# First experts of a two-layer block on one core: the up product with its operands exchanged, weights copied by VectorE, rows loaded four tiles ahead

## The reference, cut to what matters

```python
def _L0_ffn_ref(x, W1, b1, W2, b2, Wr, br):      # D, F, E = 256, 512, 8; x has 16 * 112 rows
    router_logits = jnp.einsum('bsd,de->bse', x, Wr) + br
    expert_idx = jnp.argmax(router_logits, axis=-1)
    h = jax.nn.relu(jnp.einsum('bsd,edf->ebsf', x, W1) + b1[:, None, None, :])
    y = jnp.einsum('ebsf,efd->ebsd', h, W2) + b2[:, None, None, :]
    onehot = jax.nn.one_hot(expert_idx, E, dtype=x.dtype)
    return jnp.einsum('ebsd,bse->bsd', y, onehot)
```

## Time and profile before

| | us |
|---|---|
| median of 3 runs (lowest, highest) | 850.89 (850.41, 851.85) |
| the profiled execution, its own time | 858.4 |
| span of its trace, first to last instruction | 856.7 |
| busy in the span: PE, PEld, DVE, ACT, POOL | 736.0, 543.2, 426.1, 325.7, 215.4 |
| mean granted TensorE clock, as a share of 2.4 GHz | 0.920 |

### The profile page before, as it was taken

The page is one execution under the profiler, slowest core; times in us unless marked ns, Lnnn a source line. Parts: engine busy times, 40 slices in busy tenths (PEclk is TensorE's granted clock), DMA queues, the critical chain, the costliest instruction groups (busy, mean ns, idle before and its releaser), DMA issues. The chain is left out here.

```text
span 856.7 us, 19046 instructions
## 1 busy us (share of the span) xinstructions
PE 736.0 (86%) x6340; PEld 543.2 (63%) x6341; DVE 426.1 (50%) x1316; ACT 325.7 (38%) x883; POOL 215.4 (25%) x362
## 2 busy tenths in 40 slices
PE   4589999999999999988865998873988983999996
PEld 3345667677776766665544565552766762899995
DVE  2455777777777777756621222222566764011111
ACT  2224665556555665544431322231444441111110
POOL 2301233322233233311100122222344432011111
PEclk9877999999999999999876899995999995899999
DMA  4999877788999888859332466703555531599960
GB/s 142 141 129 148 111 119 113 114 144 143 142 155 153 101 145 144 136 84 191 106 111 74 146 196 190 215 17 98 159 157 162 174 116 55 171 334 330 340 213 14
DMA packets 98086, 127.09 MB, mean 148 GB/s; under 512 B 23370, under 2 KB 82995, under 8 KB 97880
## 3 DMA queue, kind: packets, MB, share of 16 engines
q1 hardware_dynamic: 89926, 114.53, 62.4%
q0 software_dynamic: 3824, 8.46, 3.8%
q10 hardware_dynamic: 4258, 3.09, 1.5%
HBM read 74.68 MB, written 22.96 MB: 114 GB/s over the span
## 5 line engine op out<-in xcount | busy, mean ns | idle before, releaser
L491 ACT ACTIVATE probs<-psum 128x448 f32<-128x448 f32 (+2 forms) x256 | 125.4, 541 | 71.7 <-PE psum L772 70.7
L650 DVE TENSOR_REDUCE neg_max<-psum 112x2 f32<-112x750 f32 x128 | 119.0, 929 | 17.3 <-PE psum L755 15.3
L755 PE MATMUL psum<-stacks 96*128 96x487 bf16 (+1 forms) x256 | 79.7, 395 | 8.8 <-DMA stacks<-q_parts 7.5
L772 PE MATMUL psum<-stacks 102*128 102x112 bf16 (+1 forms) x1024 | 80.2, 219 | 8.0 <-DMA stacks<-mt 6.6
L772 PEld LDWEIGHTS psum<-stacks 102*128 102x128 bf16 (+1 forms) x1024 | 56.2, 101 | 40.0 <-ACT probs L491 21.3
L787 PE MATMUL psum<-probs,rings 128*32 128x112 f32 (+2 forms) x2048 | 79.5, 273 | 0.7 <-issue 0.7
L787 PEld LDWEIGHTS psum<-probs,rings 128*32 128x32 f32 (+2 forms) x2048 | 46.9, 112 | 48.7 <-issue 34.6
L1901 PEld LDWEIGHTS psum<-e_xt,rings 128*128 128x128 f32 x512 | 62.5, 200 | 2.3 <-ACT e_xt L1848 1.4
L1901 PE MATMUL psum<-e_xt,rings 128*128 128x112 f32 x512 | 62.7, 283 | 0.9 <-ACT e_xt L1848 0.9
L1915 PE MATMUL psum<-rings,e_hid 128*112 128x256 f32 x256 | 57.9, 379 | 1.3 <-DVE e_hid L1875 1.3
L1868 DVE SCALAR_TENSOR_TENSOR e_y<-psum,e_x_in 112x256 f32<-112x256 f32 x16 | 7.7, 484 | 97.9 <-PE psum L1915 97.9
(11 more groups left out here) (225 smaller groups left out, 1366.4 us busy)
## 6 DMA issues: line engine op xcount, KB each, us to landing
rings<-in_L_ffn_w SPq DMA_DIRECT2D x32, 1024.0 KB, 7.4
stacks<-rings SPq DMA_DIRECT2D x96, 243.5 KB
ct_dram<-rings SPq DMA_DIRECT2D x16, 375.0 KB, 11.0
a_ct<-ct_dram SPq DMA_DIRECT2D x16, 375.0 KB
a_ctx<-in_ctx SPq DMA_DIRECT2D x16, 375.0 KB
stacks<-q_parts SPq DMA_DIRECT2D x96, 56.0 KB
rings<-in_ctx SPq DMA_DIRECT2D x16, 256.0 KB
w<-in_L_ffn_W SPq DMA_DIRECT2D x8, 512.0 KB, 11.5
```

The costliest lines, as they stand in the source:

```text
L491: nc.scalar.activation(probs[k % 4][0:keys, :, :], src, ACT.Exp, scale=DH ** -0.5).then_inc(s["exp_done"], 1)
L650: nc.vector.tensor_reduce(neg_max[:, 0, h:h + 2], psum[0:T, pair:pair + 2, 0:S], AX, ALU.max, negate=True)
L755: last = nc.tensor.matmul(bank[2 - 2 * (k % 2) + j][0:rows, 0:KV], q_flat[n.third][0:QK, h * T:h * T + rows], k_stack[n.third][0:QK, h, :] ...
L772: last = nc.tensor.matmul(bank[4 + k % 2][0:wide, j * T:(j + 1) * T], k_flat[n.third][:, first:first + wide], q_stack[n.third][:, h, :], s ...
```

## The change

The up product exchanges its operands: the weights are stationary, the tokens move. The result then has the hidden axis on partitions and the turning back, its copy and a stage of the pipeline are gone. The stationary blocks are read from a copy `w1_now` that VectorE makes for each tile from the expert's weights (128 partitions, 1024 values), one tile ahead. The up result takes two banks of PSUM for each parity, `up` counts twice for each tile, and ScalarE makes the first half of `t_hid` after the first count. ScalarE now makes `t_hid` of tile j ahead of the copy of tile j+1. The down product, its bias and the scatter follow one step behind, not two, and there is one step less. Rows are loaded four tiles ahead into four buffers.

```diff
-        s_in = [g.sem(f"f0_tile_loaded{p}") for p in range(2)]
+        s_in = [g.sem(f"f0_tile_loaded{k}") for k in range(4)]
...
-            x_in = [tb(f"t0_in{p}", [P, ROW0]) for p in range(2)]
+            x_in = [tb(f"t0_in{k}", [P, ROW0]) for k in range(4)]
-            up = [tb(f"t0_up{p}", [P, F0]) for p in range(2)]
+            w1_now = [tb(f"t0_w1_{p}", [P, 2, F0]) for p in range(2)]
-            end = TILES + 2
+            end = TILES + 1
+            def up_bank(j, f):
+                return bank[4 * j.parity + f // 2]
...  SP
-                        if (j - 2).real():
-                            sp.wait_ge(s["x_mm"], (j - 2).count(1, 1))
+                        if (j - 4).real():
+                            sp.wait_ge(s["x_mm"], (j - 4).count(1, 1))
+                            sp.wait_ge(s["index_ready"], (j - 4).count(1, 1))
...
-                        if (j + 2).real():
-                            load(j + 2)
+                        if (j + 4).real():
+                            load(j + 4)
...  POOL
-                        if (j - 2).real():
-                            n = j - 2
+                        if (j - 1).real():
+                            n = j - 1
...  ACT
                     def step(j):
+                        if j.real():
+                            e = act.value_load(owner_i[0:1, j.at()], min_val=0, max_val=E0 - 1)
+                            if (j - 2).real():
+                                act.wait_ge(s["down"], (j - 2).count(1, 1))
+                            for f in range(K2):
+                                if f % 2 == 0:
+                                    act.wait_ge(s["up"], j.count(2, 1 + f // 2))
+                                bias = b1[:, bass.ds(e, 1), f:f + 1].rearrange("p o f -> p (o f)")
+                                nc.scalar.activation(hid[j.parity][:, f, :], up_bank(j, f)[:, f % 2 * P:(f % 2 + 1) * P], ACT.Relu,
+                                                     bias=bias).then_inc(s["hid"], 1)
                         if (j + 1).real():
                             copy_in(j + 1)
...  DVE
+                    def take_weights(j):
+                        e = dve.value_load(owner_i[0:1, j.at()], min_val=0, max_val=E0 - 1)
+                        if (j - 2).real():
+                            dve.wait_ge(s["up"], (j - 2).count(2, 2))
+                        nc.vector.tensor_copy(w1_now[j.parity][:, :, :], g.w1[:, bass.ds(e, 1), :, :].rearrange("p o k f -> p (o k) f")).then_inc(s["w1_taken"], 1)
                     def step(j):
-                        if j.real():
-                            dve.wait_ge(s["up"], j.count(1, 1))
-                            nc.vector.tensor_copy(up[j.parity][:, :], bank[j.parity][:, :]).then_inc(s["up_copy"], 1)
-                        if (j - 2).real():
-                            n = j - 2
+                        if (j + 1).real():
+                            take_weights(j + 1)
+                        if (j - 1).real():
+                            n = j - 1
...  PE
-                            e = pe.value_load(owner_i[0:1, j.at()], min_val=0, max_val=E0 - 1)
                             pe.wait_ge(s["x_copy"], j.count(1, 1))
+                            pe.wait_ge(s["w1_taken"], j.count(1, 1))
                             if (j - 2).real():
-                                pe.wait_ge(s["up_copy"], (j - 2).count(1, 1))
-                            for h in range(2):
-                                last = nc.tensor.matmul(bank[j.parity][:, :], xt2[j.parity][:, h, :],
-                                                        g.w1[:, bass.ds(e, 1), h, :].rearrange("p o f -> p (o f)"), start=(h == 0), stop=(h == 1))
-                            last.then_inc(s["up"], 1)
+                                pe.wait_ge(s["hid"], (j - 2).count(K2, K2))
+                            for f in range(K2):
+                                for k in range(2):
+                                    last = nc.tensor.matmul(up_bank(j, f)[:, f % 2 * P:(f % 2 + 1) * P], w1_now[j.parity][:, k, f * P:(f + 1) * P],
+                                                            xt2[j.parity][:, k, :], start=(k == 0), stop=(k == 1))
+                                if f % 2 == 1:
+                                    last.then_inc(s["up"], 1)
                         if (j + 1).real():
                             transpose_in(j + 1)
-                        if (j - 2).real():
-                            n = j - 2
+                        if (j - 1).real():
+                            n = j - 1
...
-                        if (j - 1).real():
-                            n = j - 1
-                            pe.wait_ge(s["up_copy"], n.count(1, 1))
-                            for f in range(K2):
-                                last = nc.tensor.transpose(bank[4 + n.parity][:, f * P:(f + 1) * P], up[n.parity][:, f * P:(f + 1) * P], g.ident[:, :])
-                            last.then_inc(s["back"], 1)
```

More of the change, by code:

```diff
@@ L1129, in ffn0 @@
         offset_i = sb("offset_i", [1, TILES], I32)
-        s = {n: g.sem("f0_" + n) for n in """b1_mm b1_made setup_mm setup_copy row_made made summed step nexts_ready padded x_mm x_copy up up_copy back back_copy down down_copy
+        s = {n: g.sem("f0_" + n) for n in """b1_mm b1_made setup_mm setup_copy row_made made summed step nexts_ready padded x_mm x_copy w1_taken up hid down down_copy
             index_ready sp_turns pool_turns""".split()}
-        s_in = [g.sem(f"f0_tile_loaded{p}") for p in range(2)]
+        s_in = [g.sem(f"f0_tile_loaded{k}") for k in range(4)]
         s_out = [g.sem(f"f0_tile_stored{p}") for p in range(2)]
@@ L1264, in tb @@
                 return g.sb(name, shape, dt, tiles)
-            x_in = [tb(f"t0_in{p}", [P, ROW0]) for p in range(2)]
-            index = [tb(f"t0_index{p}", [P, 1], I32) for p in range(4)]
+            x_in = [tb(f"t0_in{k}", [P, ROW0]) for k in range(4)]
+            index = [tb(f"t0_index{k}", [P, 1], I32) for k in range(4)]
             xt2 = [tb(f"t0_xt{p}", [P, 2, P]) for p in range(2)]
-            up = [tb(f"t0_up{p}", [P, F0]) for p in range(2)]
+            w1_now = [tb(f"t0_w1_{p}", [P, 2, F0]) for p in range(2)]
             hid = [tb(f"t0_hid{p}", [P, K2, P]) for p in range(2)]
             y = [tb(f"t0_y{p}", [P, D]) for p in range(2)]
-            end = TILES + 2
+            end = TILES + 1
+            def up_bank(j, f):
+                return bank[4 * j.parity + f // 2]
             def tile_steps(engine, step):
@@ L1315, in step @@
                         if j.real():
-                            pool.wait_ge(s_in[j.parity], j.turn(16, 16))
+                            pool.wait_ge(s_in[j.quarter], j.turn(16, 16, 4))
                             pool.sem_inc(s["pool_turns"], 1)
@@ L1348, in step @@
                     def step(j):
+                        if j.real():
[8 more added lines that the diff above has]
+                                                     bias=bias).then_inc(s["hid"], 1)
                         if (j + 1).real():
                             copy_in(j + 1)
-                        if (j - 1).real():
-                            n = j - 1
-                            e = act.value_load(owner_i[0:1, n.at()], min_val=0, max_val=E0 - 1)
-                            act.wait_ge(s["back"], n.count(1, 1))
-                            if (n - 2).real():
-                                act.wait_ge(s["down"], (n - 2).count(1, 1))
-                            for f in range(K2):
-                                bias = b1[:, bass.ds(e, 1), f:f + 1].rearrange("p o f -> p (o f)")
-                                nc.scalar.activation(hid[n.parity][:, f, :], bank[4 + n.parity][:, f * P:(f + 1) * P], ACT.Relu,
-                                                     bias=bias).then_inc(s["back_copy"], 1)
                     tile_steps(act, step)
@@ L1388, in transpose_in @@
                     def transpose_in(j):
-                        pe.wait_ge(s_in[j.parity], j.turn(16, 16))
+                        pe.wait_ge(s_in[j.quarter], j.turn(16, 16, 4))
                         if (j - 2).real():
```

28 lines of the change are left out of this document (10 added, 18 removed).

## The result

The kernel after takes 819.06 us (median of 4 runs, 816.63 to 822.54), the kernel before, run beside it, 851.37 (850.41 to 858.67, 4 runs): a ratio of 0.9606, 95% interval 0.9542 to 0.967, or 32 us less. A second set of each gave 0.9626 (0.9571 to 0.9682). The forecast was 828, with a range of 822 to 838: faster it is, but by 9 us more than forecast, and the range missed it by 3 us. The profiled execution took 822.54 us, with a span of 820.8.

What follows compares the result with a forecast made beforehand. PE, busy 86% of the span, was taken to bound the kernel, through the length of ffn0's tile loop. -6.7 - 13.7 - 6.0 + 1.3 + 2 = -23.1 us from the median 850.89 gave 828, range 822 to 838.

Steps and rivals of the forecast that it cites:

- The step of the loop: ffn0's tile loop: PE's step falls from 4.10 to 3.73 us, -6.7 us over 18 tiles.
- The late loads: ffn0's tile loop: loading rows four tiles ahead removes the waits of tiles for their rows, -13.7 us.
- The end: End of ffn0's loop: last scatter starts 6.8 us behind the last up product in place of 12.77, -6.0 us.
- The start: Start of ffn0's loop: first down product falls ahead of the third up product, which starts 1.3 us later.
- The circle through the scatter: ffn0's loop: bias add waits for the scatter two tiles back, stalling PE via the weight copy; +2 us, between 0 and 5.
- ScalarE's cover: ffn0's loop: ScalarE's copy for the next tile is seen 0.6 us before PE is free, so it costs nothing.
- the copy hidden: ffn0's loop: VectorE's weight copy, taken as 0.7 us per tile, ends before PE needs it.
- Rival B: Transfers set the pace of 12 tiles in ffn0's loop, by scatter landings or backlog: 831 to 836 us, chance 0.17.
- Rival C: Up product's pairs don't overlap as in ffn1, or ScalarE's cover is gone: 3 to 8 us less gain, chance 0.06.
- D: Loads in ffn0's loop still come late because bandwidth was short, 13.7 us stay: 839.5 us, chance 0.10.
- E: Slower: weight copy keeps GpSimd from writing its scatter's descriptors; 860 us with landings of 10 us, chance 0.05.
- these 7.5 us: The profiled execution's excess over the median of the runs; left unplaced, so the sum was taken from the median, 850.89.

Runs made afterwards that it cites:

- four_ahead: Kernel before with only its loads changed, to four buffers and four tiles ahead: 837.1 us, ratio 0.9867; 835.47 us in a later single execution.
- no_copy: Kernel after with weights copied for the first two tiles only, later tiles computed with these: 814.84 us, ratio 0.9699.
- copy_more: Kernel after with four buffers for the scattered rows and a second weight copy of 512 values per tile that nobody reads: 815.28 us, ratio 0.9667.
- peeled kernels: Kernel before with 10 tiles written out ahead of ffn0's loop, or 8 batches ahead of attention1's, in place of 6: 841.44 and 841.79 us.
- before_rows4: Kernel before with four row and four index buffers for attention1's scatter in place of two: 827.31 us, ratio 0.9799.
- before_third: Kernel before, unchanged, profiled a third time in a single execution: 852.01 us.
- before_warm: Kernel before with 30 dummy turnings filling a PE rest of 3.9 us in attention0: 844.07 us, ratio 1.0023.

## Why the prediction missed, step by step

**The step of the loop** (3.73 us, 16 pairs in 1.78, the copy in 0.7): exact. **The late loads** (-13.7): right, 13.2 by four_ahead. **The end** (-6.0): 12.77 to 6.85 is -5.9. **The start** (+1.3): +1.6. **The circle through the scatter** (+2): the place and the order of the waits were right, it cost 4.0 us, within its 0 to 5. Together -6.7 - 13.7 - 5.9 + 1.6 + 4.0 = -20.7 us, and 89.10 - 109.55 = -20.5 is measured; over all profiles of the two kernels it is -21.5 for -23.1 forecast. What the sum had too low is the landing of a scatter: 7.0 us from the earlier trace rows, and up to 8.7 measured.

**ScalarE's cover, the copy hidden**: right, no row of PE in the loop's steady part names ScalarE. **Rival B** shows in one stall. **Rival C** has fallen by the 1.78 us, **D** by four_ahead, **E** by no_copy and copy_more.

**The step that failed** is the last of the sum: "I can't place these 7.5 us; the loop is an eighth of the span, so I take the sum from the median", with a low end of 4 us "for what the timed runs may hold otherwise". It takes all phases but the loop as fixed. They aren't, even from one execution of one kernel to the next: in the profiles of before alone attention1 varies by 10 us, with PE's clock in it, and the loop by 7. Between the kernels attention0 differs by 6 in its early stretch, with one rest of PE and the clock behind it. In the profiles 5.7 us of attention0, 5.8 of attention1 and 1.4 of the gap came on top of the loop's 21.5. In attention0 the short rest is no effect of what the change computes, since both peeled kernels and before_rows4, with the old loop and other text, have it too. In attention1 it isn't the old loop, since before_third and both peeled kernels have 128 to 130 us with it. The gap's 1.4 us were not tried: 11.1 to 11.3 us with the exchanged product, 11.2 to 13.0 without it.

In the timed runs what shows is this: the two kernels as they are were 32 and 31 us apart in two sets, and 20.5 with the deeper buffers in attention1. So about 11 us of the 32 don't belong to the loop, where the prediction allowed 4 on that side. The closing sentence on precision ("tells 0.2% (1.7 us) from no change") fails for the same reason: medians of before in five sets were 851.37, 849.40, 852.54, 843.90 and 844.48 us. Beside the two low ones the kernel after was never run, so how much of the 11 us a set of its own there would show isn't known. So the kernel is faster for the reasons forecast, and by more than forecast for others; that the range was missed by 3 us only is luck, as its 4 us for everything outside the loop were a guess.

What stays open: why the 21 KB land 1.9 us later in some programs, what sets PE's clock in attention1 and at the end of attention0, and how much of attention0's 5.7 us is in the timed executions. The peeled kernels put it at 3 us (0.4%) on their chip, before_warm at nothing.

## What to carry to other kernels

A forecast made from one profiled execution has to ask in which other phases PE rests for 2 us and more, or a scatter lands late: here such a phase took up to 10 us more or less with the same work, and its part of the range should be that wide. When a small change moves the time by more than its own stage shows, compare the phases of two or three profiles of each kernel, with the granted clock of each, before looking for a mechanism in the change. If one phase swings, take its wait out of both kernels and time the pair: that showed the change's own worth here. And a load that is late costs its wait and the half clock behind it, so time ahead for loads is the first thing to try where PE rests for a tile.

## What the runs showed of the hardware that was not expected

At one place of attention0 rests of PE of 3.8 to 4.0 us were followed by 6.8 to 10.2 us at 1.2 GHz, one of 3.17 us by 3.4 us, and rests of 1.84 to 2.33 us by 3.4 us in five profiles and by none in six. 2.15 us of rest in the loop were followed by one up product at half clock. In the five profiles of the two kernels attention1 took 128.5 to 139.0 us for the same work, at granted clocks of 0.92 to 0.86. Other text in the program's later phases went with a landing of a 21 KB transfer 1.5 to 2.0 us earlier, and with a median lower by 0.4%. Executions of one kernel on one chip were up to 21 us apart (833.67 to 854.68 in 29). And an indirect scatter of 128 rows landed in up to 8.7 us in a stretch where the DMA engines are 91% busy, so two buffers behind it are too few at steps of 3.73 us.
